# Window attention block on one core: ScalarE copies before it exponentiates, and the LayerNorm steps start one slot earlier

## The reference

```
h    = layernorm(x) * g1 + b1
q,k,v = split(h @ qkv_w + qkv_b)            # 3 heads of 16 channels
attn = softmax(q*SCALE @ k^T + rel_bias)    # 64 x 64 for each head
x    = x + (attn @ v) @ proj_w + proj_b
h2   = layernorm(x) * g2 + b2
out  = x + gelu(h2 @ fc1_w + fc1_b) @ fc2_w + fc2_b
```

## Time and profile before

| | us |
|---|---|
| median of 3 runs | 1119.53 (1118.43 to 1120.45) |
| profiled execution, its own time | 1117.6 |
| its span, first to last instruction | 1115.8 |
| TensorE busy | 1055.1 (95%) |
| GpSimd busy | 759.2 (68%) |
| VectorE busy | 800.0 (72%) |
| ScalarE busy | 710.7 (64%) |
| mean granted TensorE clock | 0.984 of full speed |

### The profile page before, as it was taken

The page is one execution under the profiler, slowest core; times in us unless marked ns, Lnnn a source line. Parts: engine busy times, 40 slices in busy tenths (PEclk is TensorE's granted clock), DMA queues, the critical chain, the costliest instruction groups (busy, mean ns, idle before and its releaser), DMA issues.

```text
span 1115.8 us, 26438 instructions
## 1 busy us (share of the span) xinstructions
PE 1055.1 (95%) x7366; PEld 927.6 (83%) x7366; DVE 800.0 (72%) x2301; ACT 710.7 (64%) x1347; POOL 759.2 (68%) x1174
## 2 busy tenths in 40 slices
PE   2799999999999999999999999999899999999997
PEld 1578888888888888888888888888799999999997
DVE  3467777777777777767777777776567777777773
ACT  1356666666666666666666666666466666666664
POOL 4455677656766667766677666773778888888881
PEclk9889999999999999999999999999899999999999
DMA  1100011000111001110011100100011111111111
GB/s 34 36 15 28 28 42 35 35 28 28 42 34 37 29 28 42 34 36 29 28 41 36 36 29 28 42 29 15 15 29 42 42 42 42 42 42 40 41 40 48
DMA packets 24807, 38.25 MB, mean 34 GB/s; under 512 B 4119, under 2 KB 20698, under 8 KB 24794
## 3 DMA queue, kind: packets, MB, share of 16 engines
q1 hardware_dynamic: 24794, 38.10, 10.8%
HBM read 25.50 MB, written 12.58 MB: 34 GB/s over the span
## 4 chain that ended last, share of the span: by engine, by line
issue 34%; PE 32%; POOL 28%; DVE 2%; POOLq 1%; ACT 1%; DMA 1%; SPq 0%; DVEq 0%
PE scores_ps L592 15%; POOL rstd L374 11%; POOL lowered L461 6%; POOL centred L370 4%; PE x_ps L585 4%; POOL normed L380 3%; PE x_ps L579 3%; PE x_ps L569 3%; PE probs_t_ps L579 1%; PE probs_t_ps L585 1%; PE scores_ps L537 1%; PE mixed_ps L552 1%; POOL small L362 1%; POOL small L356 1%; POOL small L367 1%
## 5 line engine op out<-in xcount | busy, mean ns | idle before, releaser
L461 POOL TENSOR_TENSOR lowered<-biased,row_top 128x384 f32<-128x384 f32 x256 | 212.7, 831 | 270.6 <-DVE row_top L976 269.5
L786 ACT ACTIVATE probs<-lowered 128x384 f32<-128x384 f32 x256 | 134.3, 525 | 189.6 <-POOL lowered L461 188.6
L374 POOL TENSOR_TENSOR rstd<-small,minus_half 128x4 f32<-128x4 f32 (+1 forms) x160 | 243.0, 1532 | 0.0
L552 PEld LDWEIGHTS mixed_ps<-v_blocks,probs_t 128*128 128x128 f32 x1536 | 196.7, 193 | 43.2 <-ACT probs_t L767 22.7
L537 PE MATMUL scores_ps<-k_blocks,q_blocks 96*128 96x192 f32 x1024 | 226.7, 345 | 1.6 <-DVE q_blocks L964 1.6
L552 PE MATMUL mixed_ps<-v_blocks,probs_t 128*128 128x66 f32 x1536 | 210.1, 273 | 6.0 <-DVE heads L986 2.8
L972 DVE TENSOR_TENSOR biased<-scores_ps,pos 128x384 f32<-128x384 f32 x256 | 142.2, 555 | 81.6 <-PE scores_ps L537 77.3
L592 PEld LDWEIGHTS scores_ps<-wfc,hidden 128*128 128x128 f32 x1536 | 181.1, 192 | 5.7
L592 PE MATMUL scores_ps<-wfc,hidden 128*128 128x96 f32 x1536 | 179.8, 274 | 0.0
L767 ACT ACTIVATE probs_t<-probs_t_ps 128x384 f32<-128x384 f32 x256 | 125.0, 488 | 79.3 <-PE probs_t_ps L544 77.6
L537 PEld LDWEIGHTS scores_ps<-k_blocks,q_blocks 96*128 96x128 f32 x1024 | 164.7, 194 | 4.3 <-DVE q_blocks L964 2.1
(11 more groups left out here) (100 smaller groups left out, 1671.1 us busy)
## 6 DMA issues: line engine op xcount, KB each, us to landing
x_in<-in_x SPq DMA_DIRECT2D x256, 48.0 KB
x<-in_x SPq DMA_DIRECT2D x128, 96.0 KB
out<-x SPq DMA_DIRECT2D x128, 96.0 KB
pos_in<-in_L_conv_rel_bias_table SPq DMA_DIRECT2D x8, 10.6 KB
wproj<-in_L_conv_proj_w SPq DMA_DIRECT2D x6, 3.0 KB
wfc_in<-in_L_conv_fc_w SPq DMA_DIRECT2D x2, 36.0 KB
wqkv_in<-in_L_conv_qkv_w SPq DMA_DIRECT2D x2, 27.0 KB
wfc<-in_L_conv_fc_w SPq DMA_DIRECT2D x2, 24.0 KB
```

What stands on the lines that cost most here:

```text
L374: pool.tensor_tensor(rstd[:, groups], small[:, 7, groups], minus_half[:, groups], ALU.pow).then_inc(step, 1)
L461: pool.tensor_tensor(lowered[:, k % 2, :, :], biased[:, k % 2, :, :], broadcast(row_top[:, k % 2, :], 2, TOK), ALU.subtract).then_inc(lowe ...
L552: mm = pe.matmul(mixed_ps[:, at:at + MIX], probs_t[:, h, :], v_blocks[:, part, u, h, :], start=True, stop=True)
L786: act.activation(probs[:, k % 2, :, :, :].rearrange("p h a t -> p a h t"), lowered[:, k % 2, :, :].rearrange("p (a h) t -> p a h t", a=2), ...
```

## The change

Three streams are edited. ScalarE's two operations of each slot change places: the copy of slot g-2's turned probabilities comes first, the exponential of slot g-1 second, and the slot's other copies stay behind both. GpSimd's LayerNorm steps move up by one slot: the sums from slot 6 to 5, the centring from 7 to 6, the first roots from slot 0 of the next batch to slot 7, the second from 1 to 0, and the scaling from 2 to 1 (in batch 0 the steps for batch 1 stay where they were). VectorE's statistics move from slots 4 and 5 to slots 3 and 4. SP's and TensorE's streams are as they were.

```diff
--- before.py
+++ after.py
@@ -474,19 +474,22 @@
                     if first and k == 1:
                         front_sums(1)
                         front_centre(1)
-                    if k == (2 if first else 0) and not last:
+                    if first and k == 2:
                         front_root(0, 0)
                         front_root(0, 1)
-                    if k == (2 if first else 1) and not last:
+                    if k == (2 if first else 0) and not last:
                         front_root(1, 0)
                         front_root(1, 1)
-                    if k == (3 if first else 2) and not last:
+                    if k == (3 if first else 1) and not last:
                         front_scale(n + 1, 0)
                         front_scale(n + 1, 1)
+                    if k == 5 and more:
+                        front_sums(n + 2)
                     if k == 6 and more:
-                        front_sums(n + 2)
+                        front_centre(n + 2)
                     if k == 7 and more:
-                        front_centre(n + 2)
+                        front_root(0, 0)
+                        front_root(0, 1)
                     if last and k == 2:
                         back_sums(0)
                         back_centre(0)
@@ -805,12 +808,12 @@
             def body(n, first, last):
                 s0 = QUADS * n
                 for k in range(QUADS):
+                    if not (first and k < 2):
+
+                        wait(act, probs_turned, s0 + k - 1)
+                        probs_t_out()
                     if not (first and k == 0):
                         exp_of(s0 + k - 1, (k - 1) % QUADS)
-                    if not (first and k < 2):
-
-                        wait(act, probs_turned, s0 + k - 1)
-                        probs_t_out()
                     if k == 0:
                         wait(act, v_mm, 2 * n + 1)
                         v_out(0)
@@ -850,9 +853,9 @@
             k_out(0)
             batches(act, body)
             total = QUADS * BATCHES
-            exp_of(total - 1, QUADS - 1)
             act.wait_ge(probs_turned, total - 1)
             probs_t_out()
+            exp_of(total - 1, QUADS - 1)
             act.wait_ge(heads_turned, 2 * BATCHES - 1)
             heads_out(x_ps[3], 0)
             act.wait_ge(probs_turned, total)
@@ -1036,8 +1039,8 @@
                         dve.wait_ge(x2_ok, 2 * (k // 4) + 2)
                         stats_back(k // 4, 0)
                         stats_back(k // 4, 1).then_inc(stats2_ok, 1)
-                    if more and k in (4, 5):
-                        stats_front(n + 2, k - 4)
+                    if more and k in (3, 4):
+                        stats_front(n + 2, k - 3)
                     if k == 5 and not first:
                         dve.wait_ge(res_loaded, 64 * n)
                         add_proj(n - 1, x_ps[3], 0)
```

More of the change, by code:

```diff
@@ L807, in body @@
                 for k in range(QUADS):
-                    if not (first and k == 0):
-                        exp_of(s0 + k - 1, (k - 1) % QUADS)
                     if not (first and k < 2):
@@ L813, in body @@
                         probs_t_out()
+                    if not (first and k == 0):
+                        exp_of(s0 + k - 1, (k - 1) % QUADS)
                     if k == 0:
```

## The result

The changed kernel takes 1269.65 us (median of 6 runs, 1261.80 to 1277.85) against 1120.49 us of the kernel before; the ratio is 1.132 (95% interval 1.127 to 1.138). It is slower by 149 us, where 171 had been forecast. The profiled execution took 1277.85 us, the slowest of the six, so what follows shows the loss at its upper edge.

What follows compares the result with a forecast made beforehand. TensorE, busy 701.75 of 720 us, sets the pace. 28 batches x (3.1 us stall + 3.0 us clock) + 1 = 172 us on the profiled 1117.6 give 1290, stated as 1291 us for the median; range 1200 to 1335.

Steps and rivals of the forecast that it cites:

- to the landing: SP's x_in load, from first DMA issue until its data are there: taken as 10.8 us.
- period with the clock up: Loop through the x_in load and VectorE's moved statistics: 26.3 us a batch, 3.1 more than 23.19.
- the clock's share of a batch: TensorE at half speed after each idle time: 3.0 us a batch taken, bounds 1.7 and 5.1, in 28 batches.
- The load does not move with the centring: In SP's queue the x_in load stays behind the residual's four DMAs, 4.07 us after it, despite GpSimd's earlier centring.
- The stall hides the other two edits: GpSimd's 0.86 us and ScalarE's 0.3 us in slots 2 and 3 lie under VectorE's stall and count for nothing.
- GpSimd's gain of 0.86 us: TensorE's slot 3 wait for `normed` goes: 0.86 us a batch, at most 26 us over 30 batches.
- ScalarE's cost of 0.3 us: The exponential ahead of slot 2's `k_out` delays TensorE's `turn_heads`: 0.3 us a batch taken, up to 0.33.
- falls in every batch: TensorE's clock drops after the idle time in all 28 batches: 1291 us; fall in most batches, 1250 to 1330, chance 0.68.
- falls in some: TensorE's clock drops in some batches only: between 1208 and 1291 us; holding or few falls, 1205 to 1250, chance 0.18.
- the clock holds: TensorE's clock stays up, only the loop's 3.1 us count: 1208 us; holding or few falls, chance 0.18.
- The load lands sooner: x_in's data land after 8.7 us instead of 10.8: period 24.2 us, time near 1148 us; chance 0.02.
- Faster: SP issues the x_in load right after the earlier centring, leaving a gain of 0.56 us a batch: 1103 us; chance 0.03.

Runs made afterwards that it cites:

- e7: Changed kernel plus 14 unread filler matmuls on TensorE ahead of slot 4's mix in batches 1 to 30; 1201.28 us, ratio 1.072 to the kernel before.
- e5: Changed kernel with SP issuing the x_in load one turn earlier, ahead of the wait for `add_proj` and the residual's DMAs; 1109.55 us, ratio 0.990.
- e6: Changed kernel with SP issuing the x_in load behind the wait for `add_proj` but ahead of the residual's DMAs; 1111.55 us, ratio 0.993.
- e4: Kernel before with only VectorE's statistics moved to slots 3 and 4; 1277.52 us, ratio 1.135.
- e10: Kernel before with GpSimd's steps one slot earlier and the x_in load first in SP's queue, ScalarE and VectorE unchanged; 1095.49 us, ratio 0.977.
- e1: Changed kernel with VectorE's statistics put back to slots 4 and 5; 1112.59 us, ratio 0.994 to the kernel before.
- e3: Kernel before with only GpSimd's steps moved one slot earlier; 1113.32 us, ratio 0.993.
- e8: Changed kernel with the x_in load first in SP's queue and ScalarE's old order, exponential ahead of copy; 1091.95 us, ratio 0.976 to the kernel before.
- e9: Changed kernel plus 7 unread filler matmuls on TensorE ahead of slot 4's mix; 1264.93 us, ratio 1.128 to the kernel before.

## Why the prediction was right

The mechanism of the loss held step by step; ScalarE's cost was mis-sized but lies under the stall, and the clock's term was right in the mean and not batch by batch. The terms against what was measured:

| step of the sum | forecast | measured |
|---|---|---|
| residual load to x_in load | 4.07 | 4.03 |
| to the landing | 10.8 | 10.67 |
| statistics and `normalise` | 1.97 | 1.86 (511.80 to 513.66) |
| to TensorE's mix | 0.15 | 0.06 |
| that mix to the next residual load, clock up | 9.51, less 0.2 | 9.38 (e7: 526.14 to 535.52) |
| period with the clock up | 26.3 | 26.03 (e7) |
| the clock's share of a batch | 3.0 | 3.02 in the profiled execution (29.05 - 26.03), 2.4 by the medians (68.4 / 28) |
| VectorE's wait in slot 3 | 4.9 in 28 batches | 4.82 here; 4.5 to 5.3 in 22 batches, 1.4 to 2.0 in 5 |
| TensorE idle in slot 4 | 3.3 to 3.9 | 3.44 |

*The load does not move with the centring.* Right: 4.03 us behind the residual's, in the rows and by e5 and e6.

*The stall hides the other two edits.* Right, and shown by e4 (28.81 us a batch) beside the changed kernel (29.05).

*GpSimd's gain of 0.86 us.* Right in size where it can be seen: 23.26 - 22.32 = 0.94 us a batch in e10, which has the load first as well (no run has that alone). But the prediction said that it and ScalarE's cost would give 0.56 us a batch alone, 17 us. In e1 the period fell by only 23.26 - 23.10 = 0.16 us. Of the 0.40 us that are missing, 0.3 are ScalarE's mis-sized cost (next point). Another 0.17 are the load's loop through slot 4, since the period is 22.93 with the load first (e5); GpSimd's 0.08 more make up the difference. The load's loop, which the prediction left out here, shows more in e3, where it holds back 23.05 - 22.32 = 0.73 us of GpSimd's gain. The 25 waits in the earlier trace rows had said that it was close behind TensorE.

*ScalarE's cost of 0.3 us.* Mis-sized: 0.60 (e5 against e8). Slot 2's `k_out` was priced at 0.3 and measured 0.28; `tokens_out` in slot 4 was named and not priced, and costs another 0.40. It did not touch the forecast, because both lie under the stall.

*The clock.* The fall after the idle time came in most batches, not in all of the 28: after a batch with a long low stretch the next has a short wait and no fall, so the rivals "falls in every batch" and "falls in some" are mixed in one run. The low stretches were not 6.9 us each: per batch, eight were about 3.3 us, eight about 7 and six 19.5 to 23. The mean came out near the 3.0 us that was taken, in part by luck. The excess of the forecast, 171 against 149 us, is mostly here: 0.6 us a batch by the medians, 17 us; the other 5 us are the stall, 83 us in e7 where 28 x 3.1 + 1 = 88 were forecast.

Of the rivals, "the clock holds" gave 1208 us, and with the clock held by fillers the kernel takes 1201. "The load lands sooner", an estimate from the about 2 us that the Trainium skill gives for a DMA's fixed cost (DMA: Bandwidth & Descriptors, "Anatomy of one DMA — SWDGE (gpsimd) path"), did not come: the landing took 10.67 us from the first issue, within the 10.4 to 11.4 us of the kernel before. "Faster", with the load moved, forecast 1103 and is e5, 1109.6 us, less by ScalarE's mis-sized term.

## What to carry to other kernels

Before a consumer is moved ahead, find what its data's DMA is queued behind on the issuing engine, not only what frees the buffer: here the steps that free the buffer came one slot sooner, and the load still started 4.03 us behind the residual's. Where a trace already shows a short harmless wait for a load, that load's loop is the next bound, and it takes the gain of any edit elsewhere until it is moved first. A stall of a few microseconds in each turn of a loop can cost TensorE nearly as much again in clock (68 us beside 83 here), so price the idle time and what follows it apart.

## What the runs showed of the hardware

TensorE's granted clock fell in a steady loop after idle times of 1.7 to 2.4 us a batch (e9, mean clock 0.89 from 100 to 700 us) nearly as much as after 3.1 to 3.9 us (the changed kernel, 0.87), and not at all when 28 matmul passes cut the gap to under 1 us (e7, 1.00). One idle time of 1.80 us in e9 was followed by no fall.

The fall does not keep to one place. In the batch from 501.13 the clock fell some 1.9 us before the mix started (the window from 511 to 512 us averages 0.90, the next 0.50), in the batch from 184.04 some 1.1 us after its start. Having fallen, it stayed at half speed for 6.8 us in the batch from 501.13, and from 542.5 to 563.0 us, 20.5 us, in the next, though TensorE was at work without a pause in both once the mix had started. What decides between short and long was not found, and no run here tells.
